# The second layer norm's rows turned by SBUF transfers and 32x32 blocks, and a first FFN layer by token halves, in a transformer layer on one core

## The reference

```python
def attn(x):                       # x already normalized
    Q, K, V = x @ Wq.T + bq, x @ Wk.T + bk, x @ Wv.T + bv
    scores = einsum('bqd,bkd->bqk', Q, K) / sqrt(256)
    scores = scores * gaussian_mask      # one factor for each key
    return einsum('bqk,bkd->bqd', softmax(scores), V) @ Wo.T + bo
def ffn(x):                        # bw = mean(|w|, axis=1) * sign(w)
    h = gelu(einsum('bsd,hd->bsh', x, bw1) + b1, approximate=False)
    return einsum('bsh,dh->bsd', h, bw2) + b2
x = x + attn(layernorm(x))
x = x + ffn(layernorm(x))
```

## Time and profile before

| | |
|---|---|
| median of 3 runs | 1504.25 us |
| the profiled execution's own time | 1503.99 us |
| its span, first to last instruction | 1502.2 us |
| mean granted TensorE clock | 0.995 |
| PE busy | 1475.3 us, 98% |
| DVE, POOL, ACT busy | 1030.4, 834.7, 785.1 us |

### The profile page before, as it was taken

The page is one execution under the profiler, slowest core; times in us unless marked ns, Lnnn a source line. Parts: engine busy times, 40 slices in busy tenths (PEclk is TensorE's granted clock), DMA queues, the critical chain, the costliest instruction groups (busy, mean ns, idle before and its releaser), DMA issues.

```text
span 1502.2 us, 24033 instructions
## 1 busy us (share of the span) xinstructions
PE 1475.3 (98%) x9421; PEld 1330.7 (89%) x9421; DVE 1030.4 (69%) x1681; ACT 785.1 (52%) x951; POOL 834.7 (56%) x1097
## 2 busy tenths in 40 slices
PE   8999999999999999999999999999999999999997
PEld 6788989999898998989899898998989989899986
DVE  7567776767767677675776767667675677767574
ACT  5554654645556454564646546465564646546342
POOL 3564637556364673637646375573646746375553
PEclk9999999999999999999999999999999999999999
DMA  5422413224131332403314132342313324131330
GB/s 189 78 36 43 127 24 75 72 57 113 32 75 63 71 99 43 114 24 75 85 46 124 29 70 71 61 109 43 91 36 78 92 43 127 22 75 45 57 85 28
DMA packets 86060, 106.16 MB, mean 71 GB/s; under 512 B 9390, under 2 KB 77372, under 8 KB 85948
## 3 DMA queue, kind: packets, MB, share of 16 engines
q1 hardware_dynamic: 85920, 104.63, 29.3%
q10 hardware_dynamic: 28, 0.01, 0.0%
HBM read 20.72 MB, written 16.78 MB: 25 GB/s over the span
## 4 chain that ended last, share of the span: by engine, by line
PE 89%; DMA 3%; DVE 2%; SPq 2%; ACT 2%; issue 2%; POOL 1%; POOLq 0%
PE ps L886 22%; PE ps L1072 15%; PE ps L925 8%; PE ps L924 8%; PE ps L904 7%; PE ps L906 7%; PE ps L905 7%; DMA prob<-prob 2%; PE ps L872 2%; PE ps L871 2%; PE ps L870 2%; PE ps L932 2%; PE ps L853 2%; PE ps L854 2%; PE ps L856 2%; PE ps L837 2%
## 5 line engine op out<-in xcount | busy, mean ns | idle before, releaser
L319 POOL TENSOR_TENSOR ptl<-pt,pth 128x512 fp32r<-128x512 f32 x256 | 326.7, 1297 | 198.1 <-ACT pth L457 198.1
L904 PE MATMUL ps<-vh,pth 128*128 128x258 f32 x1024 | 294.2, 287 | 3.2 <-POOL ptl L319 3.2
L337 POOL TENSOR_TENSOR xin<-xin,ys 128x256 f32<-128x256 f32 x128 | 94.6, 740 | 359.0 <-DVE ys L665 358.9
L906 PE MATMUL ps<-vh,ptl 128*128 128x258 f32 x1024 | 290.7, 284 | 0.0
L905 PE MATMUL ps<-vl,pth 128*128 128x256 f32 x1024 | 289.3, 283 | 0.0
L457 ACT ACTIVATE pth<-pt 128x1024 fp32r<-128x1024 f32 x128 | 135.8, 1061 | 268.3 <-DVE pt L612 268.3
L924 PE MATMUL ps<-sgn,gh 128*128 128x256 f32 x1024 | 248.6, 281 | 5.9 <-DVE gl L647 5.9
L925 PE MATMUL ps<-sgn,gl 128*128 128x256 f32 x1024 | 248.2, 285 | 0.0
L606 DVE TENSOR_REDUCE nmax<-ps 128x1 f32<-128x1024 f32 x128 | 156.4, 1222 | 118.9 <-PE ps L886 118.9
L444 ACT ACTIVATE prob<-ps,nmax 128x1024 f32<-128x1024 f32 x128 | 142.6, 1114 | 179.7 <-DVE nmax L606 179.4
L612 DVE STREAM_TRANSPOSE pt<-prob 128x1024 f32<-128x1024 f32 x128 | 158.8, 1240 | 84.6 <-DMA prob<-prob 84.5
(11 more groups left out here) (116 smaller groups left out, 2799.8 us busy)
## 6 DMA issues: line engine op xcount, KB each, us to landing
prob<-prob SPq DMA_DIRECT2D x512, 128.0 KB, 3.4
xin<-in_L_attn_x_dram SPq DMA_DIRECT2D x32, 512.0 KB, 4.8
out_dram<-xin SPq DMA_DIRECT2D x31, 512.0 KB, 4.0
w1s<-in_L_ffn_w_dram SPq DMA_DIRECT2D x1, 1024.0 KB, 10.4
w2s<-in_L_ffn_w_dram SPq DMA_DIRECT2D x1, 1024.0 KB, 12.5
mask_bc<-mask_dram SPq DMA_DIRECT2D x1, 512.0 KB, 7.4
out_dram<-xin SPq DMA_DIRECT2D x1, 384.0 KB, 2.4
wk<-in_L_attn_Wk_dram SPq DMA_DIRECT2D x1, 256.0 KB, 5.1
```

The source lines that it names most:

```text
L319: pool.tensor_tensor(ptl[:, q % P_SLOTS, half(n)], pt[:, q % P_SLOTS, half(n)], pth[:, q % P_SLOTS, half(n)].bitcast(F32), ALU.subtract).t ...
L904: pe.matmul(with_sum, pth[:, q % P_SLOTS, tile(j)], vh[:, j, :], start=j == 0, stop=False)
L906: last = pe.matmul(with_sum, ptl[:, q % P_SLOTS, tile(j)], vh[:, j, :], start=False, stop=j == T - 1)
```

## The change

Only the batches that have a successor, 15 of 16, take the new path.

**Turning.** PE's 16 transposes a batch (L932) and their PSUM banks are gone. ACT writes the normalized rows in an order by pieces of 32 features (`xn2_keyed`); SP issues four SBUF transfers for each half of the tokens (`regroup_x2`) into the buffer that held exponentials of even tiles (`exps(0)`); DVE turns 32x32 blocks into `x2t` in SBUF (`turn_x2`), writing every fourth element. x2h is then copied from x2t, and x2l is x2t minus x2h, in x2t's own place, both inputs in SBUF.

**The first FFN layer** now goes by `hidden_pairs` in all batches, behind all of the values: pairs 0 to 3 for the first 512 tokens, 4 to 7 for the others. ACT does a gelu pair in two instructions of 512 columns.

**gl of pairs 0 and 3** moves from DVE to POOL (`lo_hidden`), between and behind the additions of b2. On POOL `rstd_ffn(7)` now stands ahead of the second half of the keys' split.

**Layouts.** xh, xl, x2h and x2l are stored by tile and then feature block; the mask on the keys becomes two DVE instructions of 512 columns for one of 1024.

```diff
+POOL_PAIRS = (0, 3)
...
-            x2h = sb("x2h", [P, C, S], F32R, place)
-            x2l = sb("x2l", [P, N2, C, HALF], F32R, place)
+            sb("gap_xn1", [P, T * D], F32, place)
+            xn2_keyed = sb("xn2_keyed", [P, N2, P // QUAD, TH, C, QUAD], F32, place)
+        with ExitStack() as place:
+            sb("gap_x2t", [P, S * C], F32, place)
+            x2t = sb("x2t", [P, N2, TH, C, P], F32, place)
+        with ExitStack() as place:
+            x2h = sb("x2h", [P, N2, TH, C, P], F32R, place)
+            x2l = sb("x2l", [P, N2, TH, C, P], F32R, place)
...
+            def regroup_x2(b, n):
+                sp.wait_ge(xn2_set, T * b + TH * (n + 1))
+                if n == 0:
+                    sp.wait_ge(p_back[(T - 2) % QUEUED], 64 * ((T * b + T - 2) // QUEUED + 1))
+                else:
+                    sp.wait_ge(x2t_set, N2 * b + 1)
+                for i in range(P // QUAD):
+                    sp.dma_start(exps(0)[i * QUAD:(i + 1) * QUAD, :],
+                                 xn2_keyed[:, n, i]).then_inc(x2_back[n], 16)
...
+                regroup_probs(b, 4)
+                for q in range(5, T):
                     regroup_probs(b, q)
+                if more:
+                    for n in range(N2):
+                        regroup_x2(b, n)
...
+            def add_b2(b, s, tiles):
+                for t in tiles:
+                    if t == 0:
                         pool.wait_ge(xn2_set, T * (b + 1))
-                    pool.tensor_tensor(xin[s][:, j, :], xin[s][:, j, :], b2_bc[:], ALU.add).then_inc(b2_added, 1)
+                    pool.tensor_tensor(xin[s][:, t, :], xin[s][:, t, :], b2_bc[:], ALU.add).then_inc(b2_added, 1)
+
+            def lo_hidden(b, k):
+                n, js = pair_of(k)
+                ts = slice(n * TH, (n + 1) * TH)
+                pool.wait_ge(gh_set, J * b + k + 1)
+                for m, j in enumerate(range(js.start, js.stop)):
+                    val = g[:, k % G_SLOTS, half(m)].rearrange("p (t c) -> p t c", t=TH)
+                    last = pool.tensor_tensor(gl[:, ts, j, :], val, gh[:, ts, j, :].bitcast(F32), ALU.subtract)
+                last.then_inc(glp_set, 1)
...
+                rstd_ffn(b, 7)
                 if more:
                     split_keys(b + 1, range(1, 2))
-                rstd_ffn(b, 7)
-                add_b2(b, s)
+                add_b2(b, s, range(TH))
+                if more:
+                    lo_hidden(b, 0)
+                add_b2(b, s, range(TH, T))
+                if more:
+                    lo_hidden(b, 3)
...
+            def hi_rows_ffn(b, n):
+                if b < B - 1:
+                    act.wait_ge(x2t_set, N2 * b + n + 1)
+                    act.activation(x2h[:, n], x2t[:, n], ACT.Copy).then_inc(x2h_set, 1)
...
+                    by_dve, by_pool = splits_up_to(b, k - G_SLOTS)
+                    act.wait_ge(gl_set, by_dve)
+                    if by_pool:
+                        act.wait_ge(glp_set, by_pool)
...
+                act.activation(xn2_keyed[:, q // TH, :, q % TH].rearrange("p i c r -> p c i r"),
+                               xin[s][:, q, :].rearrange("p (c i r) -> p c i r", c=C, r=QUAD),
...
+                normalize_ffn(b, s, 5)
                 hi_keys(b + 1, range(1, 2))
-                normalize_ffn(b, s, 5)
                 hi_queries(b + 1, range(2, QG))
+                hi_rows_ffn(b, 0)
                 normalize_ffn(b, s, 6)
-                hi_rows_ffn(b, 0, slot(0))
                 normalize_ffn(b, s, 7)
-                hi_values(b + 1, range(0, 3))
-                hi_rows_ffn(b, 1, slot(1))
-                hi_values(b + 1, range(3, VG))
+                hi_values(b + 1, range(VG))
                 load_table(b, ACT.Gelu)
-                for j in range(J):
-                    hidden_ready(b, j)
-                    act.activation(two(g[:, j % G_SLOTS, :]), slot(2 - j % 2), ACT.Gelu, bias=cols[:, j:j + 1],
-                                   scale=alpha1[:, j:j + 1]).then_inc(gelu_set, 1)
+                gelu_pairs(b, range(0, 1))
+                hi_rows_ffn(b, 1)
+                gelu_pairs(b, range(1, J))
...
+                rows = from_banks(slot(n))
+                for c in range(C):
+                    last = dve.scalar_tensor_tensor(
+                        out=kmf[:, c, half(n)].rearrange("p (t q) -> p t q", q=P), in0=rows[:, :, c, :], scalar=1.0,
+                        in1=mask_bc[:, half(n)].rearrange("p (t q) -> p t q", q=P), op0=ALU.add, op1=ALU.mult)
+                last.then_inc(km_set, 1)
...
+            def turn_x2(b, n):
+                dve.wait_ge(x2_back[n], 64 * (b + 1))
+                dve.transpose(x2t[:, n].rearrange("p t c (q g) -> p g (t c) q", g=P // QUAD),
+                              exps(0).rearrange("p (g k r) -> p g k r", g=P // QUAD, r=QUAD)).then_inc(x2t_set, 1)
+
+            def lo_rows_ffn(b, n):
                 dve.wait_ge(x2h_set, N2 * b + n + 1)
-                dve.tensor_tensor(part, banks, x2h[:, :, half(n)].bitcast(F32),
+                dve.tensor_tensor(x2l[:, n], x2t[:, n] if b < B - 1 else from_banks(slot(0)), x2h[:, n].bitcast(F32),
...
                 n, js = pair_of(k)
                 ts = slice(n * TH, (n + 1) * TH)
                 val = g[:, k % G_SLOTS, :].rearrange("p (m t c) -> p m t c", m=2, t=TH)
-                split_hidden(b, k, gh[:, ts, js, :].rearrange("p t m c -> p m t c"),
-                             gl[:, ts, js, :].rearrange("p t m c -> p m t c"), val)
+                hi = gh[:, ts, js, :].rearrange("p t m c -> p m t c")
+                dve.wait_ge(gelu_set, J * b + k + 1)
+                dve.tensor_copy(hi, val).then_inc(gh_set, 1)
+                if pool_splits(b, k):
+                    return
+                dve.wait_ge(gh_set, J * b + k + 1)
+                dve.tensor_tensor(gl[:, ts, js, :].rearrange("p t m c -> p m t c"), val, hi.bitcast(F32),
+                                  ALU.subtract).then_inc(gl_set, 1)
...
+                turn_x2(b, 0)
                 lo_queries(b + 1, range(2, QG))
                 add_attention(b, s, 7)
-                lo_rows_ffn(b, 0, x2l[:, 0], slot(0))
-                lo_values(b + 1, range(0, 3))
-                lo_rows_ffn(b, 1, x2l[:, 1], slot(1))
-                lo_values(b + 1, range(3, VG))
+                lo_rows_ffn(b, 0)
+                lo_values(b + 1, range(VG))
                 dve.wait_ge(kl_set, N2 * (b + 2))
-                for j in range(J):
-                    split_column(b, j)
+                turn_x2(b, 1)
+                split_pair(b, 0)
+                lo_rows_ffn(b, 1)
+                for k in range(1, J):
+                    split_pair(b, k)
...
                 if q == 1 and not first:
-                    pe.wait_ge(gelu_set, J * b)
+                    pe.wait_ge(gelu_set, J * (b - 1) + J - 1)
...
+                        if more and r == 0 and j % 2 == 0:
+                            by_dve, by_pool = splits_up_to(b, (J + j) // 2)
+                            pe.wait_ge(gl_set, by_dve)
+                            pe.wait_ge(glp_set, by_pool)
...
+                        if b < B - 1:
+                            pe.wait_ge(km_set, N2 * (b + 2))
+                    if k == 1 and b < B - 1:
+                        pe.wait_ge(vl_set, VG * (b + 1) + 2)
...
-                pe.wait_ge(km_set, N2 * (b + 1) + 1)
-                turn_rows_ffn(b, 0, 0)
-                values(b + 1, range(0, 3))
-                pe.wait_ge(km_set, N2 * (b + 2))
-                turn_rows_ffn(b, 1, 2)
-                values(b + 1, range(3, VG))
-                for j in range(J):
-                    if j == 0:
-                        pe.wait_ge(vl_set, VG * (b + 1) + 2)
-                    if j >= 2:
-                        pe.wait_ge(gelu_set, J * b + j - 1)
-                    order = [(c, lo, n) for c in range(C) for lo in (False, True) for n in range(N2)]
-                    if j == 0:
-                        order.sort(key=lambda cpn: cpn[2])
-                    for k, (c, lo, n) in enumerate(order):
-                        if j == 0 and k % 4 == 0:
-                            pe.wait_ge(x2l_set, N2 * b + n + 1)
-                        last = pe.matmul(ps[:, 4 - 2 * (j % 2) + n, :], sgn1[:, c, tile(j)],
-                                         x2l[:, n, c, :] if lo else x2h[:, c, half(n)],
-                                         start=c == 0 and not lo, stop=c == C - 1 and lo)
-                    last.then_inc(hidden, 1)
+                values(b + 1, range(VG))
+                hidden_pairs(b, range(J))
```

More of the change, by code:

```diff
@@ L176, in preln_attention_ffn @@
         p_back = [sem(f"p_back{k}") for k in range(QUEUED)]
+        x2t_set, glp_set = (sem(n) for n in ("x2t_set", "glp_set"))
+        x2_back = [sem(f"x2_back{n}") for n in range(N2)]
         stats2, aggr2, vareps2, rstd2_set, xn2_set, b2_added = (
@@ L197, in tile, with from_banks, pool_splits, splits_up_to @@
```

(40 more changed lines are left out.)

53 lines of the change are left out of this document (18 added, 35 removed).

## The result

| | before | changed |
|---|---|---|
| median, 4 runs each | 1504.26 us | 1551.65 us (1548.38 to 1553.69) |
| ratio to before | | 1.031, interval 1.029 to 1.0331 |
| span of the profiled execution | 1502.2 us | 1549.6 us |
| mean granted TensorE clock | 0.995 | 0.979 |

The change makes the kernel 3.1% slower. The forecast was 1531, its range ended at 1549; the direction was right, the size 20.7 us short.

The account below looks back on a forecast made before the run. PE's instruction stream was taken as the bound: 1503.99 us, with 2.06 a batch removed but stalls of 3.6 and some 0.2 added, net 1.8 a batch, 27 in 15, gave 1531 us; range 1488 to 1549.

Parts of the forecast that it names:

- What was removed: PE's transposes, slower value matmuls behind them and a wait for x2l go: 2.06 us a batch, 30.9 in 15.
- The lock on tile 7's first step: POOL's first step on the last tile stands behind DVE's x2l of the first half, ending 0.9 us late.
- The block transpose at 1.25: DVE's transpose into x2t, every fourth element written, on the chain to x2h: priced at 1.25 us.
- rival C: The strided write takes DVE's block transpose to 2.3 us, all from x2h on 1.05 later: 1547 us; chance 0.11.
- The clock behind the stall: No clock term; PE's stall at pair 3, waiting for gelu 1, was priced at its length, 2.2 us a batch.
- The turns: DVE and POOL alternate over the first layer's hidden values, each blocking the other; PE stalls 0.8 and 0.5 us a batch.
- rival A: DVE and POOL's turns over the hidden values cost nothing, second layer 0.64 us early: 1494 us; chance 0.28.
- The mask at zero: Keys' mask in two DVE instructions ahead of ql: effect on the queries' wait taken as zero.
- The layouts' matmuls at nothing: PE's matmuls on the new layouts, runs of 128 columns: no extra cost; 0.01 us on each would be 13 us.
- the 0.3 before pair 2 and at the second layer: PE waits 0.1 us for gelu 0 before pair 2 and some 0.2 before the second layer's third tile.

Follow-up runs that it names:

- e5: Changed kernel with x2l of the first half ahead of the last add_attention on DVE: 1534.34 us, ratio 1.0201.
- e2: Changed kernel with the block transpose writing 32 elements in a row, FFN outputs added to the wrong tokens: 1539.0 us, ratio 1.0234.
- e7: Kernel before, with block transposes of 1024 and 512 columns at several write steps added at its end; one execution, total not comparable.
- e9: Changed kernel with 12 idle matmuls between pairs 2 and 3 and all gl on DVE: 1528.59 us, ratio 1.0162.
- e1: Changed kernel with all eight gl of a batch on DVE, none on POOL: 1545.62 us, ratio 1.0277.
- e3: Changed kernel with 12 idle matmuls on PE between pairs 2 and 3: 1550.48 us, ratio 1.0304.
- e6: Changed kernel with the next batch's first tile of scores between pairs 2 and 3, not behind pair 7: 1563.71 us, ratio 1.0389.
- e8: Changed kernel with the next batch's first scores between pairs 2 and 3 and all gl on DVE: 1493.23 us, ratio 0.9921.
- e4: Changed kernel with the mask on the keys in one DVE instruction of 1024 columns, as before: 1548.22 us, ratio 1.0294.
- e11: e8 with x2l of the first half early as in e5 and the mask in one instruction as in e4: 1481.4 us, ratio 0.9844.
- e12: e11 with the block transpose written in a row and gelu putting the tokens in order, as in e10: 1481.82 us, ratio 0.984.
- e10: Changed kernel with the block transpose written in a row and gelu reading PSUM at every 32nd element, full computation: 1533.95 us, ratio 1.02.

## Why the prediction was right in direction and short in size

- **What was removed**: right. Turning takes 25.6 us less between PE's starts, and values and three pairs take 11.42 from tile 7's end to where PE stands, as worked out (11.43).
- **The lock on tile 7's first step**: right. 1.07 where 1.06 was forecast (1009.74 to 1010.8), and e5 removes it. The Trainium skill, "SBUF — State Buffer", section "Who interferes with whom", has a lock under which the loser blocks wholly; these rows agree: a step of 0.2 waits for the end of a 1.2 us instruction.
- **The block transpose at 1.25**: the step that failed first. It takes 2.02, by rival C's mechanism and somewhat under its 2.3. I had refused it since no row showed it and taken the nearest row, of an operation that writes in a row. The stall was to end 13.63 behind tile 7 and ended at 14.37: 0.74 late, and 0.77 is the transpose: 11 us in 15 batches. Without it the kernel is 12.6 faster (e2); that the two numbers are so close is partly chance, as fewer batches at half pace and new waits also stand in e2. The Trainium skill's same page, section "Specifications (TRN2)", has 16-byte lines that want two hits for full pace; e7 agrees: free at two hits a line, dearer at one.
- **The clock behind the stall**: not a term of the sum at all, and the larger miss. 1.64 in the batch shown, in 13 of 15 batches, some 21 us; e9 against e1 gives 17.0, where half pace stood in 9. I had priced a stall of PE at its length; this one cost 2.95 + 1.64.
- **The turns**: right as a mechanism (gl 1.51, CAST 1.07, POOL's gl 1.87, so A is out), and DVE comes to its maximum 31.65 behind tile 7 where 31.08 was forecast. Wrong in the sum: their stalls of 0.8 and 0.5 a batch, 19.5 us, are not there, since PE comes to pair 7 late by then. So the time has these turns at nothing, as rival A had it, but not for A's reason. They show only where PE is kept busy: 22 us in e3 against e9, 70 in e6 against e8, the latter with a half clock of its own. That the forecast came within 21 us is in part luck: these 19.5 us too many stood against the clock's 21 that were not in it.
- **The mask at zero**: not shown to be wrong. The queries' wait for ql grew by 6.0, and no run isolates why; e4 takes 2.8 of it back, but the wait differs by as much between kernels with the same mask (6.1 to 8.7).
- **The layouts' matmuls at nothing**: right; before the stall they keep 0.23.

In the forecast's own terms, over 15 batches: 27, and 11 (transpose), 21 (clock), -19.5 (turns that are covered), -3 (the 0.3 before pair 2 and at the second layer, of which 0.09 was there) and 6 (queries) make 42.5. The span grew by 47.4. Of the 5 that are left, 4.3 lie in the matmul steps of the second layer (2.7) and the scores (1.6); their cause is open.

## What to carry to other kernels

A stall of the engine that bounds a kernel is not priced at its length: look at the granted clock behind such a stall, and at the work further down that the stall hides, since both change when it goes. So single edits may show little or a loss (e1: 6, e3: 1, e6: -12) where a pair is worth 58 us (e8) or 23 (e9); when a stall is filled with real work, ask what that work used to cover. And an operation is priced by a row of its own access pattern: a transfer-and-block route off PE pays only once the chain it makes is behind other work (e8, e11, e12).

## What the runs showed of the hardware

- DVE's 32x32 block transpose of float32 costs nothing more at every second element (1.25, 0.71) and 1.5 to 1.6 times as much at every fourth (1.08 for 0.71; 2.02 for 1.24). ACT's gelu reading PSUM at every 32nd element took 774 ns, as in a row.
- Behind 2.8 us without a matmul, TensorE's granted clock was at the 1.2 GHz level for 3 us or more in 13 of 15 batches of the change, but in only 9 and 10 behind the same stall in e1 and e4, and in 11 behind 3.0 us in e6; behind 2.0 us (e2, e5, e10) in 6, 5 and 7; behind at most 0.6 (e3) in none. In each run with 2.0 us or more, the same stall brings the clock down in some batches and not in others.
- A CAST of one input also takes part in the turns with POOL: 1.07 on average where it is 0.69 alone.
